# Token shift by transfers within SBUF, a second buffer for the transposed input, and feed-forward steps at later places, in two attention networks

## What is computed

```python
def shift_token(t):
    t1, t2 = jnp.split(t, 2, axis=-1)
    t2 = jnp.pad(t2, ((0, 0), (1, 0), (0, 0)))[:, :-1]
    return jnp.concatenate([t1, t2], axis=-1)

def _layer(x, ...):
    q, k, v = jnp.split(shift_token(x) @ wqkv, 3, axis=-1)    # to heads of 64
    q, k = rotary_xpos(l2norm(q) * qs, l2norm(k) * ksc)
    x = x + local_attention(q, k, v) @ wo
    h = shift_token(x)
    h = (h - mean(h)) / sqrt(var(h) + 1e-5) * lg + lb
    a, g = jnp.split(h @ w1 + b1, 2, axis=-1)                 # hidden 341
    return x + (a * gelu(g)) @ w2 + b2
```

## Time and profile before

| | us |
|---|---|
| median of three runs | 8491.79 (8490.57 to 8493.28) |
| span of the profiled execution | 8494.7 |
| L0f, from its first to its last `fshift` | 714 to 4711 |
| L1f, the same | 5782 to 6713 |
| TensorE busy, share of the span | 6835.9, 80% |
| VectorE, ScalarE, POOL busy | 5625.5, 4984.1, 4201.7 |

### The profile page before, as it was taken

One profiled execution on the slowest core, in us unless ns is written; L12 is line 12 of the kernel. 1 busy time (PEld: TensorE's weight loads), 2 busy tenths in 40 slices (PEclk: granted clock), 3 DMA queues, 4 the chain that ended last, 5 costly groups with the idle time before them and its releaser, 6 DMA issues. The chain is left out here.

```text
span 8494.7 us, 243140 instructions
## 1 busy us (share of the span) xinstructions
PE 6835.9 (80%) x92628; PEld 4768.7 (56%) x92628; DVE 5625.5 (66%) x11929; ACT 4984.1 (59%) x10706; POOL 4201.7 (49%) x3732
## 2 busy tenths in 40 slices
PE   5777999999999999999999499987888577633267
PEld 2325666666666666666666388874555333223245
DVE  6895776777677677777677367665666588745432
ACT  4545777777778777777777344435767554302122
POOL 4555665666666566666566244454444355430000
PEclk9888999999999999999999699998999788866578
DMA  3321111111111111111111200001000132331001
GB/s 125 121 96 52 41 38 51 38 40 51 40 38 52 41 38 48 42 40 46 44 40 40 70 5 5 5 5 29 15 23 15 40 125 121 137 79 57 21 0 30
DMA packets 234164, 413.22 MB, mean 49 GB/s; under 512 B 41944, under 2 KB 125360, under 8 KB 214128
## 3 DMA queue, kind: packets, MB, share of 16 engines
q1 hardware_dynamic: 225344, 377.76, 14.1%
q10 hardware_dynamic: 1584, 15.21, 0.4%
q0 software_dynamic: 6144, 5.25, 0.4%
HBM read 208.61 MB, written 32.18 MB: 28 GB/s over the span
## 5 line engine op out<-in xcount | busy, mean ns | idle before, releaser
L763 POOL TENSOR_TENSOR L0f_qr<-L0f_qs,L0f_table 128x512 f32<-128x512 f32 x776 | 990.5, 1276 | 459.0 <-ACT L0f_qs L804 356.3
L1018 PE MATMUL L0f_ring<-L0f_wqkv,L0f_hT 128*128 128x512 f32 x2324 | 1172.7, 610 | 42.2 <-ACT L0f_hT L799 37.5
L770 POOL TENSOR_TENSOR L0f_qr<-L0f_qr,L0f_m 128x512 f32<-128x512 f32 x776 | 985.7, 1270 | 162.2 <-issue 106.9
L834 ACT ACTIVATE L0f_scores<-L0f_scores,L0f_nmx,L0f_rn 128x64 f32<-128x64 f32 x3072 | 985.3, 401 | 132.2 <-DVE L0f_nmx L939 131.0
L1075 PEld LDWEIGHTS L0f_o<-L0f_pT,L0f_vmix 64*64 64x64 f32 x18480 | 759.2, 136 | 158.6 <-issue 135.7
L1075 PE MATMUL L0f_o<-L0f_pT,L0f_vmix 64*64 64x32 f32 x18480 | 801.5, 221 | 48.8 <-ACT L0f_pT L842 32.1
L1075 PE MATMUL L0f_o<-L0f_pT,L0f_vb 64*64 64x32 f32 x6160 | 750.8, 221 | 0.9 <-issue 0.8
L777 POOL TENSOR_TENSOR L0f_qr<-L0f_qr,L0f_rn 128x512 f32<-128x512 f32 x388 | 396.7, 1044 | 687.6 <-DVE L0f_rn L931 686.3
L908 DVE TENSOR_TENSOR L0f_m<-L0f_ring,L0f_table 128x512 f32<-128x512 f32 x776 | 524.0, 686 | 253.6 <-ACT L0f_qs L804 244.7
L1075 PEld LDWEIGHTS L0f_o<-L0f_pT,L0f_vb 64*64 64x64 f32 x6160 | 604.3, 137 | 0.9 <-issue 0.8
L916 DVE TENSOR_REDUCE L0f_ssq<-L0f_sq 128x8 f32<-128x512 f32 x776 | 509.7, 676 | 76.7 <-ACT L0f_sq L809 71.8
(11 more groups left out here) (538 smaller groups left out, 17144.5 us busy)
## 6 DMA issues: line engine op xcount, KB each, us to landing
L0f_vmix<-L0f_vb SPq DMA_DIRECT2D x768, 128.0 KB, 2.5
L0a_bc_all<-L0a_bc_rows SPq DMA_DIRECT2D x32, 2048.0 KB, 11.3
L2a_bc_all<-L2a_bc_rows SPq DMA_DIRECT2D x32, 2048.0 KB, 11.2
L0f_vmix<-L0f_vb SPq DMA_DIRECT2D x672, 64.0 KB, 2.0
L1f_vmix<-L1f_vb SPq DMA_DIRECT2D x96, 128.0 KB, 2.3
L0f_wqkv<-L_ffn_wqkv_dram SPq DMA_DIRECT2D x7, 1536.0 KB, 6.2
L2f_parts<-L2f_zero ACTq DMA_DIRECT2D x8, 1088.0 KB, 11.5
n_s<-mixer_out SPq DMA_DIRECT2D x32, 256.0 KB, 5.1
```

The source lines that it names most:

```text
L763: e.tensor_tensor(rotated, qs[:, q % QN], spread(cos, 1, 8), ALU.mult).then_inc(cosed.sem, 1)
L770: e.tensor_tensor(rotated, rotated, m2[:, q % SN], ALU.add).then_inc(added.sem, 1)
L834: a = e.activation(s_ps[:, s, h, j], s_ps[:, s, h, j], ACT.Exp, bias=nmx[:, s, col:col + 1], scale=rn[:, tt, 2 * u, col:col + 1])
L1018: e.matmul(bank[:], hT[:, tt * P:tt * P + P], wqkv[:, layer % 2, col:col + 512], start=True, stop=True).then_inc(full, 1)
```

## The change

It does the following in both networks, shown for L0f. The diff below is cut; L1f's differs in `SIDE`, which is shown too.

- `shift` is four transposes of `xs`, `fshift` has no step on TensorE any more: VectorE's statistics and ScalarE's normalisation read `xf`. `xs` and `xf` are filled by SP with three DMAs each, from SBUF to SBUF, the upper channels one partition lower. POOL's copy is gone, and so are `xb` and VectorE's copy to `xn`.
- `hT` has two buffers, and ScalarE's copy to it waits for the projections of tile 3 of the sequence before.
- the places in `SIDE` and two planned durations in `TOOK` are new; `LATER` stays. The ring has one use fewer per sequence.
- SP's order per sequence: `fetch`, mix 0, `feed`, mix 1 to 3 in L0f; `fetch`, `feed`, mix 1 to 3 in L1f.

```diff
-    SIDE = [(("fshift",), (0, 1)), (("fturn",), (0, 2)), (("gate", 0), (1, 0)), (("gate", 1), (1, 0)),
-            (("gate", 2), (1, 0)), (("fetch",), (1, 2)), (("up", 0), (1, 1)), (("layer",), (2, 1)), (("shift",), (2, 1)),
-            (("up", 1), (1, 2)), (("up", 2), (2, 2)), (("down",), (3, 2))]
+    SIDE = [(("fshift",), (0, 2)), (("fturn",), (1, 1)), (("gate", 0), (1, 2)), (("gate", 1), (1, 2)),
+            (("gate", 2), (2, 0)), (("up", 0), (2, 1)), (("layer",), (2, 1)), (("shift",), (2, 1)),
+            (("up", 1), (2, 2)), (("up", 2), (3, 0)), (("down",), (3, 2))]
...
-    TOOK = {"score": 1.5, "value": 1.3, "flip": 1.0, "turn": 0.6, "proj": 0.95, "out": 0.25 * pairs, "shift": 1.5, "fshift": 1.0,
-            "fturn": 0.6, "gate": 0.95, "up": 0.95, "down": 2.8, "fetch": 0.0, "layer": 0.0, "end": 0.0}
+    TOOK = {"score": 1.5, "value": 1.3, "flip": 1.0, "turn": 0.6, "proj": 0.95, "out": 0.25 * pairs, "shift": 0.5, "fshift": 0.0,
+            "fturn": 0.6, "gate": 0.95, "up": 0.95, "down": 2.8, "layer": 0.0, "end": 0.0}
...
-    RING = ("shift", "proj", "turn", "out", "fshift", "fturn", "gate", "up", "down")
+    RING = ("shift", "proj", "turn", "out", "fturn", "gate", "up", "down")
...
-        xb = r.sb("xb", [P, TT + 1, C])
-        hT = r.sb("hT", [P, SEQ])
+        xs = r.sb("xs", [P, TT, C])
+        xf = r.sb("xf", [P, TT, C])
+        hT = r.sb("hT", [P, 2, SEQ])
...
+                def fetch(it, b):
+
+                    e.wait_ge(*x2_ready(it, ("down",), x2_ready.per))
+                    e.sem_inc(passed, 1)
+                    e.wait_ge(*ring.written(it, ("shift",), 1))
+                    e.sem_inc(passed, 1)
+                    tile0 = sequence(("shift",), b) * TT
+                    e.dma_start(xs[:, :, 0:DH], g.f[:, tile0:tile0 + TT, 0:DH]).then_inc(fetched, 16)
+                    e.dma_start(xs[1:P, :, DH:C], g.f[0:P - 1, tile0:tile0 + TT, DH:C]).then_inc(fetched, 16)
+                    e.dma_start(xs[0:1, 1:TT, DH:C], g.f[P - 1:P, tile0:tile0 + TT - 1, DH:C]).then_inc(fetched, 16)
+
+                def feed(it, b):
+
+                    for done in furthest(*[ring.read(it, ("out", tt), ago(("fshift",), ("out", tt))) for tt in range(TT)]):
+                        e.wait_ge(*done)
+                        e.sem_inc(passed, 1)
+                    e.wait_ge(*xn_ready(it, ("down",), 1))
+                    e.sem_inc(passed, 1)
...
+                def mix_all(it, b):
+                    fetch(it, b)
+                    mix(it, 0)
+                    feed(it, b)
+                    for tt in range(1, TT):
                         mix(it, tt)
...
                         if kind == "shift":
 
-                            for done in ring.all_written(it, [s for s in uses if s[0] == "proj" and s[1] == TT - 1]):
+                            for done in ring.all_written(it, [s for s in uses if s[0] == "proj" and s[1] == TT - 1], 1):
                                 e.wait_ge(*done)
                             e.wait_ge(*ring.written(it, step))
-                            e.activation(hT[:], ring.at(step)[:], ACT.Copy).then_inc(ring.empty_of(step), 1)
+                            e.activation(hT[:, buffer_of(it, step)], ring.at(step)[:], ACT.Copy).then_inc(ring.empty_of(step), 1)
...
                         elif kind == "xn":
+                            e.wait_ge(*ring.written(it, ("fturn",), 1))
                             e.wait_ge(*rstd_ready(it, ("down",)))
                             for tt in range(TT):
-                                a = e.activation(xn[:, tt], xn[:, tt], ACT.Identity, bias=shifted[:, tt:tt + 1],
+                                a = e.activation(xn[:, tt], xf[:, tt], ACT.Identity, bias=shifted[:, tt:tt + 1],
                                                  scale=rstd[:, tt:tt + 1])
...
                         elif kind == "fshift":
 
                             e.wait_ge(*ring.written(it, ("fturn",), 1))
-                            e.wait_ge(*ring.written(it, step))
-                            e.tensor_copy(xn[:], ring.at(step).rearrange("p (t c) -> p t c", t=TT)).then_inc(ring.empty_of(step), 1)
-                            e.drain()
+                            e.wait_ge(fed_in, 48 * (it + 1))
                             for tt in range(TT):
-                                e.bn_stats(stats[:, tt], xn[:, tt])
+                                e.bn_stats(stats[:, tt], xf[:, tt])
...
                         if kind == "shift":
                             if l is None:
                                 e.wait_ge(zeroed, 1)
-                            e.wait_ge(*xb_ready(it, ("fetch",)))
+                            e.wait_ge(fetched, 48 * (it + 1))
                             for tt in range(TT):
-                                cols = slice(tt * P, tt * P + P)
-                                e.matmul(bank[0:DH, cols], xb[:, 1 + tt, 0:DH], g.ident[:], start=True, stop=True)
-                                e.matmul(bank[DH:P, cols], xb[:, 1 + tt, DH:C], g.down1[:], start=True, stop=False)
-                                a = e.matmul(bank[DH:P, cols], xb[:, tt, DH:C], g.last1[:], start=False, stop=True)
+                                a = e.transpose(bank[:, tt * P:tt * P + P], xs[:, tt], g.ident[:])
...
-        SIDE = [(("fshift",), (0, 1)), (("fturn",), (1, 0)), (("gate", 0), (1, 0)), (("gate", 1), (1, 0)),
-                (("gate", 2), (1, 0)), (("fetch",), (0, 2)), (("up", 0), (1, 1)), (("layer",), (2, 1)), (("shift",), (2, 1)),
-                (("up", 1), (1, 1)), (("up", 2), (3, 0)), (("down",), (3, 2))]
+        SIDE = [(("fshift",), (0, 2)), (("fturn",), (1, 1)), (("gate", 0), (1, 2)), (("gate", 1), (1, 2)),
+                (("gate", 2), (2, 0)), (("up", 0), (2, 1)), (("layer",), (2, 1)), (("shift",), (0, 2)),
+                (("up", 1), (2, 2)), (("up", 2), (3, 0)), (("down",), (3, 2))]
```

More of the change, by code:

```diff
@@ L414, in lag @@
         kind = step[0]
-        if kind in ("fetch", "layer", "shift"):
+        if kind in ("layer", "shift"):
             return -1
@@ L492, in pool_events @@
             return found
-        if kind in ("fetch", "layer", "end"):
+        if kind in ("layer", "end"):
             return [(0.0, step)]
@@ L497, in pool_events @@
         return []
[L499 removed]
+    PLAIN = {"exp": 1.5, "exp_gap": 0.7, "unflip": 0.3, "ocopy": 0.3, "xn": 0.3, "act_ring": 0.2, "copy": 0.2, "square": 1.0, "ssq": 2.0, "rot": 1.2, "newton":
              3.0, "max": 0.2, "norm": 5.0, "norm_gap": 2.0, "unflip_dve": 0.5, "dve_ring": 0.3, "cos": 1.0, "add": 2.5,
@@ L703, in _ @@
                     first, last = l * BATCH, l * BATCH + BATCH - 1
+                    fetch(first, 0)
                     mix(first, 0)
+                    feed(first, 0)
                     mix(first, 1)
@@ L742, in body @@
                         kind = step[0]
-                        if kind == "fetch":
-                            e.wait_ge(*x2_ready(it, ("down",), x2_ready.per))
-                            e.wait_ge(*ring.written(it, ("shift",), 1))
-                            e.sem_inc(passed, 1)
-                            e.tensor_copy(xb[:, 1:, :],
-                                          g.f[:, bass.ds(sequence(step, b) * TT, TT), :]).then_inc(xb_ready.sem, 1)
-                        elif kind == "layer" and last:
+                        if kind == "layer" and last:
                             e.wait_ge(table_ready, 1 if l is None else l + 1)
@@ L953, in body @@
                             if step[1] == 0:
-                                e.wait_ge(*xb_ready(it, ("fetch",), 1))
+                                e.wait_ge(*ring.written(it, ("shift",), 1))
                             e.wait_ge(*ring.written(it, step))
```

113 lines of the change are left out of this document (62 added, 51 removed).

## The result

The changed kernel takes 9410.9 us (median of four runs, 9385.99 to 9428.1), the kernel before 8492.2: a ratio of 1.108, 95% interval 1.1066 to 1.1094, or 919 us more. The direction is the predicted one; 9411 lies far above 8788 and outside the range. The profiled execution has a span of 9384.2 us, 890 above the one of before.

A forecast was written before the change was run, and what follows sets the result against it. TensorE was taken to bound L0f (467 of 500 us busy, 83.3 us per sequence). Per sequence 2.4 - 2.0 + 4.1 + 2.0 = 6.5 us, by 48 +312, L1f -24, open feeds +8: +296 on 8491.79, so 8788, range 8590 to 8910.

The forecast's parts named there:

- Added transfers: Six SP transfers per sequence, priced from vmix: landing 2.5 us after issue (2 to 6), feed hidden with 3.6 to spare.
- Rival (d): Both traps, and the clock falls twice or transfers land 4 us later than vmix: 8920 and more, chance 0.06.
- fetch: free: The fetch on SP's queue goes out after x2 with 50 us until shift, so it costs nothing.
- bounds 4 if feed lands late: Upper bound on tile 0's delay in L0f, forecast as 2.4 us, should the feed land late.
- First trap: POOL: L0f: rstd between cos k and cos q waits for VectorE's statistics and delays rotations; tile 0 ends 2.4 us later.
- flip (0,1): Flip of tile 0, group 1, in L0f's traced sequence: expected at 2478.7 against 2476.32, TensorE waiting 1.2 us there.
- Second trap: ScalarE: L0f: exp 7 between gates makes four table loads per sequence, not two; TensorE waits 3.2 us, 4.1 in all.
- Clock: L0f: TensorE's new hole of 4.8 + 1.2 us lowers the granted clock: 2.0 us per sequence, within 0 to 4.4.
- Sum: L0f 6.5 us per sequence by 48, +312; L1f -24; open feeds after the main loops +8: +296, giving 8788.
- Removed: Work and waits of shift, fshift and hT leave each sequence: about 4.5 us of 83.3 if nothing else moved.
- (a): Neither trap bites because queues run otherwise than planned: -4.3 us by 48 in L0f, 8270, chance 0.08.
- (c): Only POOL's trap bites, not ScalarE's: 2.4 - 2.0 + 2.0 = 2.4 us per sequence, 8607, chance 0.10.

The follow-up runs named there:

- E5: Changed kernel with the feed as one transfer of whole rows (127 pieces of 2 KB as written) plus the 0.8 KB one, VectorE copying the lower half over; 9721.8 us.
- E9: Changed kernel with each transfer of 127 partitions cut into one of 112 and one of 15, both networks; 8914.7 us.
- E6: Changed kernel without the fetch's transfers: TensorE transposes the rows as they stand, ScalarE shifts by one column in two copies, both networks; 9195.8 us.
- E7: Kernel before with only the new SIDE places of L0f; shifts stay on TensorE, one buffer, no transfer; 8910.8 us.
- E12: E9 with ScalarE's squares placed ahead of the second gate in L0f; POOL's root not moved; 8774.3 us.
- E10: E9 with POOL's root behind both additions and ScalarE's squares ahead of the second gate in L0f; 8375.6 us.
- E14: Kernel before with L0f's new places, POOL's root behind both additions and ScalarE's squares ahead of the second gate, no transfer; 8473.4 us.
- E13: E9 with POOL's root behind both additions in L0f; ScalarE's squares not moved; 8598.8 us.
- E8: Kernel before with the attention's shift as four transposes, ScalarE's copy in two halves and two hT buffers, both networks, no transfer; 8427.5 us.
- E11: E9 with L0f's SIDE back in the places of the kernel before, L1f keeping the new ones; 8559.4 us.

## Why the prediction was wrong, point by point

- **Added transfers**: this is the step that failed. It priced the landing from vmix, 2.5 us (2 to 6) after the issue, and found it "hidden, with 3.6 us to spare". Measured: 10.2 us from the first issue, and 4.7 us late in leaving. vmix was the wrong row to go by: its difference from the new transfers was put down to the run of 256 B instead of 2 KB, and the number of partitions, 127, was never looked at. Of the 623 us between 8788 and 9411, 496 are this step. Rival (d), "8920 and more", a chance of 0.06, holds the measured time and had the transfers late by 4 us, but by their 256 B pieces, a cause that E5 and E9 rule out: it holds 9411 by luck. "fetch: free" failed as well: without it the kernel takes 215 us less (E6, both networks). The "bounds 4 if feed lands late" were too near, as the feed came 10 us later than written, not one or two.
- **First trap: POOL**: the mechanism was right in every link, and its signs came (POOL idle 4.1 us before the root in E9). With the feed on time the wait for the rotation's bank is 4.3 us per sequence (E9) and 3.9 without transfers (E7); predicted 4.8. For flip (0,1) behind it I had 1.2, and it is 0.5 (22.0 us over 42).
- **Second trap: ScalarE**: right, gate 3.1 (predicted 3.2), hT 0.6 (0.5), four loads per sequence instead of two. The Trainium skill, "ScalarE: Activation LUTs", section "What ACT_TABLE_LOAD costs", gives 1283 ns for the load and about 2.66 us for a switch with its drain. The loads here agree with the first (1283 ns); with the second the waits would have been longer than 3.1, so the row was the better price.
- **Clock**: under-sized. I took 2.0 us per sequence within 0 to 4.4, for POOL's hole. POOL's trap alone costs 4.4 (E12 against E10), both traps 4.7 with the transfers (E9 against E10) and 3.2 without them (E7 against E14: 81.87 and 78.67 us busy). I gave the second hole nothing, but ScalarE's trap alone costs 1.9, and its clock is 0.97 (E13), POOL's 0.93 (E12).
- **Sum**: had the transfers landed as written, the forecast of 8788 would have stood against E9's 8915, 127 us short and outside the range by 5. By place: L0f grew by 367 us, where I had 312; L1f by 19, where I had -24; and the stretch between the loops by 33, most of it in L1a, where I had 8 for the open feeds of both networks. So the clock's missing 2.7 us per sequence, 130 us, is more than L0f's miss of 55: the other terms there came to some 75 us too much. In the changed kernel L1f lost 171 us, because there the statistics stand ahead of a normalisation, so that TensorE waits up to 10.1 us for the probabilities whenever the feed is late:

```profile
PE L1f_pt L1886 <- DVE L1f_prob L1775: 152.6, 18, 10.1
DVE L1f_stats L1792 <- DMA L1f_xf<-f: 119.2, 16, 9.2
```
- **Removed**: 4.5 us per sequence was the wrong size for what can be had. E8 took the shift's 1.45 and `hT`'s 0.78 and gave back 1.6 of the 2.2, with one ScalarE copy more.
- **Rivals**: (a), 8270 without traps, is nearest to E10, which has no trap and the fast transfer: 8376. For such a kernel, which the change did not make, the direction was right and the size 106 us too good. (c) left out L1f's -24 and the open feeds' +8: by its own terms it is 8591, not 8607, still inside the range.

What stays open: why the transfer behind one of 127 partitions is held 6.2 to 6.6 us while those after it, and the one of 0.8 KB ahead, are not. With 127 pieces of 2 KB as written it was held 4.1 us, so the hold goes neither by the bytes nor by the pieces alone. That the 83 us are the clock is read from TensorE's busy times; no run holds the clock fixed. And why L1a takes some 30 us longer beside the transfers is open.

## What to carry to other kernels

Price an added transfer from a row with the same number of partitions, not only the same bytes or length of run. Look at the DMA share while it flies, and cut a transfer with an awkward count (127) into parts that spread (112 and 15). When steps of a planned order move, read off the new order of every queue and undo each bad neighbour before judging the move: the same places gave +421 us, -21 with two planned times changed (E14), or -119 with these and the transfers made fast (E10). Where TensorE is the bound, a hole costs its own length and the slower clock behind it; here 4.7 us beside 6.6 of waits.

## What the runs showed of the hardware that I had not expected

- A transfer between SBUF tensors of 127 partitions moved 18 GB/s with 0.08 of the 16 engines busy; the same bytes as 112 and 15 partitions, in the same 256 B pieces and at the same offset, were moved at up to 167 GB/s with the other transfer of the feed beside them (0.61 busy, 2614 to 2616 us of E9) and cost 496 us less in all.
- The transfer issued next behind it holds the issuing queue 6.2 to 6.6 us instead of 0.6, whatever its own size (0.8 KB, or a vmix of 64 to 128 KB), so the cost falls on work that has nothing to do with it.
- ScalarE's copy of 64 partitions by 512 takes 0.60 us, as long as that of 128 partitions: halving the partitions saves nothing (E8: 592 to 602 ns each, against 597).
- Cut into 112 and 15, the whole feed, 1023 pieces of 256 B and 255 KB, was in 4.2 us behind its first issue (E11: issued at 2546.67, the statistics that wait for it start at 2550.90); with 127 partitions it took 10.2.
